# Splitting every expert weight block during self-attention, in a float32 layer on one core

## The reference

```python
x = x + xattn(layernorm(x), ctx_1024)     # feats(4*512) @ W_qv over 1601 context rows
x = x + attn(layernorm(x))                # 16 heads of 32, causal, @ Wm + bm
x = x + ffn(layernorm(x))

# ffn
logits = x @ w_router.T; probs = softmax(logits)
expert_weight, expert_idx = top_k(probs, 2); expert_weight /= sum(expert_weight)
# every row goes to its 2 experts of 8
inter = square(relu(einsum('ecd,efd->ecf', binned, w1_stack)))   # w1 (8, 512, 512)
outb  = einsum('ecf,edf->ecd', inter, w2_stack)                  # w2 (8, 512, 512)
moe   = scatter_add(outb * weight)
shared = square(relu(x @ ws1.T)) @ ws2.T                         # 512 -> 1024 -> 512
return shared + moe
```

## Time and profile before

| | us |
|---|---|
| median of 3 runs | 1294.9 (1294.11 to 1295.1) |
| the profiled execution | 1293.87 |
| its span | 1292.2 |
| TensorE busy (matmul) | 1268.4 |
| VectorE busy | 750.5 |
| ScalarE busy | 357.9 |
| GpSimd busy | 169.4 |

### The profile page before, as it was taken

The page is one execution under the profiler, slowest core; times in us unless marked ns, Lnnn a source line. Parts: engine busy times, 40 slices in busy tenths (PEclk is TensorE's granted clock), DMA queues, the critical chain, the costliest instruction groups (busy, mean ns, idle before and its releaser), DMA issues.

```text
span 1292.2 us, 21499 instructions
## 1 busy us (share of the span) xinstructions
PE 1268.4 (98%) x7571; PEld 830.9 (64%) x7572; DVE 750.5 (58%) x1404; ACT 357.9 (28%) x632; POOL 169.4 (13%) x173
## 2 busy tenths in 40 slices
PE   6999999999999999999999999999999999999999
PEld 4344444444444444457888888898986777777743
DVE  4456555645455554478887888756535544444456
ACT  2322212212121211225444544441312323223200
POOL 1000000000000000003001104503324100000055
PEclk9999999999999999999999999999999999999999
DMA  9999999999999999812566753132779887786397
GB/s 354 411 418 415 415 416 418 419 419 418 419 413 404 393 398 403 310 58 111 192 268 261 294 189 120 44 122 98 260 247 313 241 253 228 229 251 189 101 349 249
DMA packets 115379, 371.76 MB, mean 288 GB/s; under 512 B 11264, under 2 KB 33792, under 8 KB 111104
## 3 DMA queue, kind: packets, MB, share of 16 engines
q1 hardware_dynamic: 110208, 354.33, 72.7%
q0 software_dynamic: 5120, 16.78, 3.7%
HBM read 332.54 MB, written 58.20 MB: 302 GB/s over the span
## 4 chain that ended last, share of the span: by engine, by line
PE 92%; DMA 4%; DVE 2%; SPq 1%; issue 1%; ACT 0%; POOL 0%; ACTq 0%; POOLq 0%; DVEq 0%
PE ps L2026 14%; PE ps L1914 13%; PE ps L2098 12%; PE ps L2088 10%; PE ps L2381 5%; PE ps L1989 4%; PE ps L1872 3%; PE ps L2479 2%; PE ps L2471 2%; PE ps L2004 2%; PE ps L2397 2%; PE ps L2400 2%; PE ps L2403 2%; PE ps L2390 2%; PE ps L2387 2%; PE ps L2384 2%
## 5 line engine op out<-in xcount | busy, mean ns | idle before, releaser
L2026 PE MATMUL ps<-arena 128*64 128x512 f32 (+1 forms) x832 | 192.6, 595 | 0.0
L1914 PE MATMUL ps<-arena 128*64 128x512 f32 (+1 forms) x1024 | 177.5, 503 | 2.1 <-DMA arena<-ctx_t 1.3
L2098 PE MATMUL ps<-split 128*128 128x256 f32 x1344 | 170.7, 285 | 1.1 <-DVE split L1381 1.1
L2098 PEld LDWEIGHTS ps<-split 128*128 128x128 f32 x1344 | 163.7, 191 | 5.6 <-issue 3.5
L809 ACT ACTIVATE arena<-ps 128x512 f32<-128x512 f32 (+2 forms) x132 | 67.2, 523 | 340.4 <-PE ps L1989 180.2
L1914 PEld LDWEIGHTS ps<-arena 128*64 128x64 f32 x1024 | 65.1, 137 | 121.9 <-issue 119.2
L2026 PEld LDWEIGHTS ps<-arena 128*64 128x64 f32 (+1 forms) x832 | 58.4, 137 | 112.9 <-issue 112.2
L1278 DVE SCALAR_TENSOR_TENSOR arena<-arena,hbar 128x512 f32<-128x512 f32 x128 | 90.5, 749 | 67.8 <-PE ps L1989 66.3
L2088 PE MATMUL ps<-split 128*128 128x512 f32 x384 | 96.7, 401 | 1.1 <-DVE arena L1449 1.1
L1252 DVE TENSOR_TENSOR F<-arena,ps 128x512 f32<-128x512 f32 x16 | 11.0, 688 | 135.9 <-ACT split L854 135.9
L712 POOL TENSOR_TENSOR arena<-arena,row_b 128x512 f32 (+1 forms) x16 | 20.2, 1268 | 475.8 <-DVE arena L1152 448.0
(11 more groups left out here) (245 smaller groups left out, 1999.7 us busy)
## 6 DMA issues: line engine op xcount, KB each, us to landing
arena<-ctx_t SPq DMA_DIRECT2D x122, 800.5 KB, 16.6
arena<-ctx_n SPq DMA_DIRECT2D x96, 768.0 KB, 13.2
arena<-ctx_n SPq DMA_DIRECT2D x32, 1024.0 KB, 14.2
split<-parts_low SPq DMA_DIRECT2D x26, 768.0 KB
high<-parts_low SPq DMA_DIRECT2D x39, 512.0 KB
moe_in<-zero SPq DMA_DIRECT2D x3, 3328.0 KB, 13.6
low_late<-parts_low SPq DMA_DIRECT2D x13, 768.0 KB
moe_out<-arena SPq DMA_DIRECT2D x39, 256.0 KB, 3.0
```

Of the source, the lines that this page charges most:

```text
L1914: last = mm(bank(n)[S * h:S * (h + 1), 0:w], qT[:, k, S * h:S * (h + 1)], ctxT[h][:, k, at_j:at_j + w], start=(k == 0), stop=(k == KD - 1))
L2026: last = mm(bank(7)[S * h:S * (h + 1), :], ET[0:w, c, S * h:S * (h + 1)], ctxN[h][0:w, c, :], start=(c == 0), stop=(c == JC - 1))
L2098: last = mm(dst[:, 2 * P * m:2 * P * (m + 1)], w[a][:, k, c], tokens[b][:, k, :], start=(k + i == 0), stop=(k == KD - 1 and i == 2))
```

## The change

All four k blocks of w1 and w2 of every expert are split in stage B: 16 whole sets of 2048 columns (`NS = 2 * E`). There are three staging places (`NB = 3`) and three sets per pair of row tiles, in the pairs n = 1 to 5; of every three sets VectorE subtracts two and GpSimd the third (a new `low_of_set` on GpSimd, behind `add_bm`). The zeroing is cut into 13 pieces. SyncE's order per set is new: it loads the next raw block before it stores.

```diff
-KA, KB = 3, 2
-NS = E + E // 2
+NS = 2 * E
+NB = 3
+ZEROED = 13
-RAW_TILES = 5
...
             for n in range(NS):
                 sp.wait_ge(high_done, n + 1)
-                store_part(n, parts_high, stage_high)
-                sp.wait_ge(low_done, n + 1)
-                store_part(n, parts_low, stage_low)
-                sp.wait_ge(parts_out, 32 * (n + 1))
+                if n > 0:
+                    sp.wait_ge(parts_out, 32 * n)
                 if n + 2 < NS:
                     load_raw(n + 2)
-                if n in (3, 5, 7):
-                    sp.wait_ge(pool_filled, ZERO)
-                    zero_slots((n - 3) // 2)
...
+                store_part(n, parts_high, stage_high)
+                if n % NB == 2:
+                    sp.wait_ge(low_pool, n // NB + 1)
+                else:
+                    sp.wait_ge(low_done, n + 1 - (n + 1) // NB)
+                store_part(n, parts_low, stage_low)
+                if 1 <= n <= ZEROED:
+                    if n == 1:
+                        sp.wait_ge(pool_filled, ZERO)
+                    zero_slots(n - 1)
...
+            def low_of_set(n):
+                i = n % NB
+                pool.wait_ge(high_done, n + 1)
+                nc.gpsimd.tensor_tensor(stage_low[i], stage_raw[i][:, :, :], stage_high[i].bitcast(F32), ALU.subtract
+                                        ).then_inc(low_pool, 1)
-            with pool.Fori(0, T) as t:
+            for t in range(T):
                 add_bm(t)
+                if t >= 5 and t % 2 == 1 and NB * ((t - 3) // 2) - 1 < NS:
+                    low_of_set(NB * ((t - 3) // 2) - 1)
```

```diff
-            def load_low(g):
-
-                i = g % 3
-                if g >= 3:
-                    sp.wait_ge(low_back[i], 16 * (g // 3))
-                sp.dma_start(low_w[i].bitcast(F32).rearrange("p k n -> p (k n)"),
-                             parts_low[0][bass.ds(expert_of[g] * P, P), :], cond=other_expert(g)
-                             ).then_inc(low_back[i], 16)
+            def load_low(g, parts, places, back):
+
+                odd, e = group[g] >= E, group[g] & (E - 1)
+                if g > 0:
+                    sp.wait_ge(back, 16 * g)
+                sp.dma_start(all_high[:, bass.ds(places[0] + odd * (places[1] - places[0]), KD * D)].bitcast(F32),
+                             parts[bass.ds(e * P, P), :], cond=group[g] != group[g - 1] if g > 0 else None
+                             ).then_inc(back, 16)
...
+            def three_passes(dst, parts, high_w, low_w, waits):
+
                 waits[0]()
-                for k in range(n):
-                    mm(dst, parts[0][:, k, :], high_w(k), start=False, stop=False)
+                for k in range(KD):
+                    mm(dst, parts[0][:, k, :], high_w(k), start=(k == 0), stop=False)
                 waits[1]()
-                for k in range(n):
+                for k in range(KD):
                     mm(dst, parts[1][:, k, :], high_w(k), start=False, stop=False)
                 waits[2]()
-                for k in range(n):
-                    last = mm(dst, parts[0][:, k, :], low_w_of[:, k, :], start=False, stop=(k == n - 1))
+                for k in range(KD):
+                    last = mm(dst, parts[0][:, k, :], low_w(k), start=False, stop=(k == KD - 1))
                 return last
```

More of the change, by code:

```diff
@@ L222, in perceiver_layer @@
         assert used[0] == WS
[L223 to L227, removed]
+        stage_low, stage_high = ([split[:, at[part]:at[part] + KD * D].rearrange("p (k n) -> p k n", n=D)
+                                  for at in stage_at] for part in range(2))
+        assert free_b <= stage_at[0][0] and stage_at[-1][1] + KD * D <= ARENA
         at(WS)
@@ L265, in perceiver_layer @@
         v0, v1, e0, e1, s0f, s1f, vs = (carve(T) for _ in range(7))
-        nt, st0, st1, cnt = (carve(E) for _ in range(4))
-        eg_f = carve(GT)
+        nt, st0, st1, cnt, some = (carve(E) for _ in range(5))
+        iota_odd = carve(E // 2)
+        eg_f, rank, turn = (carve(GT) for _ in range(3))
         assert used[0] <= 4 * KD * D, used[0]
@@ L1097, in _ @@
             experts(0, True, False, True)
[L1098 to L1104 removed]
+            with act.Fori(1, GT - 1) as g:
                 experts(g, True, True, True)
@@ L1534, in stage_b @@
                     attn_low(a - 2, 0)
-                if last and more:
-                    low_of_set(2 * n - 1)
-                elif last:
+                if last and more and NB * n < NS:
+                    low_of_set(NB * n - 2)
+                elif last and not more:
                     norm_factors(7, 0, TR)
@@ L2412, in experts, with at_place @@
-            def experts(g, now=None, last=None, second=False, whole=True):
-                if last is not None:
+                for k in range(KD):
+                    last = mm(dst, parts[0][:, k, :], low_w(k), start=False, stop=(k == KD - 1))
+                return last
+            def at_place(places, odd):
+                lo = places[0] + odd * (places[1] - places[0])
+                return lambda k: all_high[:, bass.ds(lo + k * D, D)]
+            def experts(g, now=True, last=True, second=False):
+                if last:
@@ L2450, in _, with expert @@
+            def expert(g):
+                group = pe.value_load(eg_i[0:1, bass.ds(g, 1)], min_val=0, max_val=2 * E - 1)
+                return group & (E - 1), group >= E
+            pe.wait_ge(w1_in, 16 * 6)
             pe.wait_ge(relu_ready, 4 * (TA // 2) - 2)
-            experts(0, now=(0, 0))
+            experts(0, last=False)
             shared_second(TA // 2 - 1, 0)
             shared_last(TA // 2 - 1)
-            experts(1, now=(1, 0), last=0, second=True)
-            for g in range(2, RAW_TILES):
-                experts(g, now=(g % 3, g // 3), last=(g - 1) % 3)
@@ L2457, in _ @@
-            with pe.Fori(1, (GT - 3) // 3) as n:
+            experts(1, second=True)
+            with pe.Fori(0, (GT - 3) // 3) as n:
                 for i in range(3):
-                    experts(3 * n + i + 2, now=((i + 2) % 3, n + (i + 2) // 3), last=(i + 1) % 3, whole=False)
-            experts(GT - 1, now=((GT - 1) % 3, (GT - 1) // 3), last=(GT - 2) % 3, whole=False)
-            experts(GT, last=(GT - 1) % 3)
+                    experts(3 * n + i + 2)
+            experts(GT - 1)
+            experts(GT, now=False)
```

255 lines of the change are left out of this document (91 added, 164 removed).

## The result

| | us |
|---|---|
| before, median of 4 runs | 1294.63 (1294.11 to 1295.1) |
| after, median of 4 runs | 1303.34 (1302.53 to 1303.82) |
| after to before, with its 95% interval | 1.0075 (1.0063 to 1.0087) |
| the profiled execution after, and its span | 1303.82, 1302.1 |

The account below looks back on a forecast made before the run. TensorE, busy 1268.4 of 1292.2 us, was taken as the bound. From 1293.87 us, 16.9 gained with the experts and 8.25 plus 0.5 lost in self-attention gave 1285.7, stated as 1286.3 us to allow for the median; range 1278 to 1294.

Parts of the forecast that it names:

- expert stage: Expert loop and its start: outer products save 13.5 us, first five inner products 0.9, start 1.1 and 1.4; 16.9 in all.
- 1.4 us ahead of tile 0: Start of the experts: TensorE's wait, perhaps for tile 0's last weights, goes; 1.4 us taken, 0 to 1.4 possible.
- 1.1 for the low part: Expert tile 1: TensorE's 1.1 us wait goes, as the low half is skipped when tiles 0 and 1 share an expert.
- register instructions: Expert tiles: 16 instead of 10 ahead of the passes, taken at 0, at most 10.8 us; as a rival 1296.5, chance 0.12.
- lock: Self-attention: GpSimd's subtraction blocks VectorE's maxima subtraction on shared ports; TensorE stands 1.65 us in five pairs, 8.25 us (6.8 to 11.5).
- first pair: Self-attention: VectorE's first subtraction grows by 0.53 us with no room in its chain, costing 0.5 us once.
- DMA of the same stretch: Self-attention: 11.8 MB a pair at 410 GB/s take 28.8 us, raw blocks come 9 us or more early; cost nothing.
- rival: Self-attention: transfers become the bound, late raw blocks hold ScalarE; 370 GB/s, 36.2 us a pair, 1299 us (1294 to 1303); chance 0.10.

Follow-up runs that it names:

- stores first: Changed kernel, but SyncE issues both stores of a set before waiting for the set before and loading; 1284.41 us, 0.9932 to before.
- stores first + later: Changed kernel with both stores issued before the wait and GpSimd's subtraction held until VectorE has passed the row maxima; 1278.80 us, 0.9890 to before.
- zeroing behind: Changed kernel with all 13 zeroing transfers issued after the last set; 1284.98 us, 0.9940 to before; with GpSimd's subtraction also held back, 1278.29 us.
- four pieces: Changed kernel with both stores issued before the wait and GpSimd's subtraction made in four 512-column instructions; 1279.07 us, 0.9893 to before.
- subtraction later: Changed kernel, but GpSimd's subtraction waits until VectorE has subtracted the row maxima; 1300.66 us, 1.0050 to before.
- float32 outer product: Changed kernel with four float32 passes in place of six rounded ones in each tile's outer product, results differ; 1316.54 us, 1.0180 to before.

## Why the prediction was wrong

- **The expert stage was right.** Of the 16.9 us forecast, 15.5 lie between the two marks (13.5, 0.9 and 1.1), and 15.8 came there. The float32 passes of the outer product were sized at 13.5 and measured at 13.1 to 13.2 by putting them back. The 1.4 us ahead of tile 0 lie before the first mark and became 0.5. The 1.1 for the low part became 0.3; a wait of 1.1 for ScalarE stands where 0.9 was before. In all 16.7 us came.
- **The register instructions cost nothing**, as taken: tiles of 5.91 to 5.99 us, with 5.98 forecast without them, leave no room.
- **The lock was right in mechanism, place and size.** GpSimd was put at 4.6 us and took 4.61. The subtraction of the maxima was to be 2.1 us late and was 2.0 longer; TensorE was to stand 1.65 us in each of five pairs, and stood 1.36 to 1.54 where the queue was cured. Its price in the full kernel: 5.6 us (stores first against stores first + later, where some went to the queue) to 6.7 us (zeroing behind with and without), against 8.25.
- **The first pair** lost 1.0 us and not 0.5: pair 1 is 2.4 us longer, 1.37 of it the lock.
- **"DMA of the same stretch", cost at nothing, was the step that failed.** The bytes were right (11.8 MB a pair). The 410 GB/s were a rate of 2 us; the full queue moved 364 over a pair and 380 over 33 us with the four pieces, near the rival's 370; that is 31.1 to 32.4 us of transfer a pair and not 28.8. That alone was no loss: with the stores first the pairs keep to 32.65 us. Wrong was the raw block's lead: "a raw block is issued two ahead, after one landing: by this placing 9 us or more before its turn". The landing was read as 4.0 us, of the low store, which had the queue nearly to itself. The same trace has the high parts' stores of the same 1024 KB at 7.7 us. In the changed kernel SyncE puts a load, two stores and a zeroing into the queue together. They share the engines, and the low store lands 12.6 us after its issue. So one landing is a whole period, the period is 13.8 us, and three sets take 41.4 us where a pair has 32.65. ScalarE first stood for a raw block at 672.63 (2.37 us), in pair 3, and TensorE behind it in pairs 4 and 5.
- **The rival named it, at 0.10, and was mis-sized the same way.** It had 1.4 us of open queue per set, and about 4 us were measured; 36.2 us a pair, and 41.4 were measured. Its 1299 was 4 us short, 1294 to 1303 its range. That its number came so near is partly luck: 41.4 a pair would make 43.8 us over five pairs by its own sum, but the queue lengthened two pairs only, and the stage lost 17.2 us to it. The argument against it, "the zeroing stands behind each store and fills such gaps", is what the rows turn round: the zeroing is issued right behind the store and shares the engines with it, the gap stays, and each period is 2.3 us longer with it. Moving it away alone won 16.9 us in self-attention.
- **The clock had no term.** 5.8 us of the loss came from half clock behind waits of 3.1 us or more. They are part of what the queue cost: with the stores first the clock is 1.000.

In sum: self-attention was forecast at +8.75 and came at +26.2. Curing the queue alone takes 17.2 us off that stage; with the zeroing behind and the lock cured too 8.1 more go, and 0.9 us above the old stage remain.

The Trainium skill, "DMA: Bandwidth & Descriptors", section "Rules for kernel authors", says to issue a transfer early and to wait on its semaphore late, since the fixed setup cost then overlaps. By that rule SyncE's order was the place to look at: the changed loop waits first and issues next, and the run with the stores first bears the rule out, 17.2 us less in the stage. The same page of the Trainium skill, section "Where 436 GB/s comes from", has a memory-side limit of about 358 GB/s, weighed in the prediction. With this one core at work it is not borne out: 374 GB/s were measured over 28 us, and the page of the profile before shows up to 419 over slices of 32 us in cross-attention. The measurement decides.

## What to carry to other kernels

In this kernel a queue that is filled in bursts, behind a wait for the last burst, had a period of its own: the hole and the time of the bytes (13.8 us with 3.94 MB, 11.5 with 3.15). Work it out for the loop as it will be, with all transfers of a turn in the queue at once, and set it against the time that the consumer leaves; a landing time read while the queue was nearly empty did not carry over (4.0 us against 12.6). Two costs on one path hide each other: in self-attention curing the lock alone won 3.6 us and curing the queue alone 16.9 to 17.2, but both won 21.8 to 25.3. An elementwise instruction on GpSimd with two operands in SBUF belongs where VectorE has none of that kind, or in short pieces: both were tried here, and with the stores first they won 4.6 and 6.7 us of the stage.

## What was not expected of the hardware

TensorE's granted clock fell to 0.50 behind idle stretches of 3.1 to 3.6 us (behind the one that ended at 736.57 it was 0.50 to 739, 0.86 from 739 to 742 and 1.00 from 742); behind idle stretches of 1.4 to 1.7 us it stayed at 1.00. So a wait of 3.6 us here cost up to 5.2. It did not always fall at once: behind the wait that ended at 715.44 it was 0.66 for 1.56 us and then 0.50. Shorter waits in other runs were followed by it as well: 2.74 us with the subtraction later (0.67, then 0.50 from 741.20 to 743.20), and 2.22 us with the float32 outer product (1.00 for 1.08 us, then 0.54 from 713.77 to 716). Behind 1.87 us in that run it stayed at 1.00.

Of VectorE's three instructions in a row there, only the subtraction with two SBUF operands was held by GpSimd. In the run with the stores first GpSimd was at work from 686.07 for 4.61 us. The instruction before, which reads one operand from PSUM (at 686.07, 1.21 us), and the one with a single input (at 687.32, 1.22 us) kept their time.
